# Deformable-convolution kernel: patches of 8 rows by 3 columns, hats made once per unit on compact rows and spread by transfers

## The reference, cut to what matters

```python
def _L1_conv_ref(x, w_off, b_off, w_def):      # x: group-normed input
    x = jax.nn.relu(x)
    offset = conv(x, w_off, 3x3, pad 1) + b_off        # 18 channels: (dy, dx) of 9 taps
    py = base_y + off[:, :, 0]                         # where each tap samples, per pixel
    px = base_x + off[:, :, 1]
    samp = _bilinear_gather(x, py, px)                 # 4 neighbours, bilinear weights, zero outside
    return jnp.einsum('bckhw,ock->bohw', samp, w_def)  # 9 taps x 128 channels -> 128 channels
x = x + _L1_conv_ref(_gn(x), w_off, b_off, w_def)
```

## Time and profile before

| what | us |
|---|---|
| median of 3 runs (2178.71 to 2181.53) | 2181.06 |
| the profiled execution: its span, which is its own time here | 2179.7 |
| first block | 0 to about 334 |
| first sampling product / last one | 386.8 / 2165.0 |
| PE busy over the span | 1802.6 (83%) |
| DVE | 1796.7 (82%) |
| ACT | 1445.8 (66%) |
| POOL | 1014.2 (47%) |

### The profile page before, as it was taken

The page is one execution under the profiler, slowest core; times in us unless marked ns, Lnnn a source line. Parts: engine busy times, 40 slices in busy tenths (PEclk is TensorE's granted clock), DMA queues, the critical chain, the costliest instruction groups (busy, mean ns, idle before and its releaser), DMA issues.

```text
span 2179.7 us, 38860 instructions
## 1 busy us (share of the span) xinstructions
PE 1802.6 (83%) x11347; PEld 1181.0 (54%) x11348; DVE 1796.7 (82%) x2778; ACT 1445.8 (66%) x1922; POOL 1014.2 (47%) x798
## 2 busy tenths in 40 slices
PE   5999993788888888888888888888888888888888
PEld 4877772455555555555555555555555555555545
DVE  6888875888888888888888888888888888888885
ACT  3555553677777777767676777767777767676764
POOL 2555562544444444444444444444444444444442
PEclk9999995899999999999999999999999999999999
DMA  4334332111111111111111111111111111111100
GB/s 123 116 115 120 113 90 70 43 47 43 47 47 47 47 47 47 47 44 40 45 47 47 47 46 39 47 47 47 47 47 47 47 47 46 36 47 47 47 21 20
DMA packets 129048, 120.23 MB, mean 55 GB/s; under 512 B 9257, under 2 KB 112311, under 8 KB 129015
## 3 DMA queue, kind: packets, MB, share of 16 engines
q1 hardware_dynamic: 129015, 119.82, 18.5%
HBM read 80.53 MB, written 35.71 MB: 53 GB/s over the span
## 4 chain that ended last, share of the span: by engine, by line
DVE 34%; issue 21%; PE 19%; ACT 12%; POOL 10%; DVEq 1%; ACTq 1%; DMA 0%; POOLq 0%; SPq 0%
DVE hats L1168 11%; PE bank L692 10%; ACT z L866 8%; DVE samples_lo L1178 5%; POOL weights L1466 5%; PE bank L713 5%; DVE offs L1196 5%; DVE rest L1213 4%; POOL x_bo L1421 3%; ACT dist L889 3%; DVE parts L1212 3%; DVE parts L1216 2%; PE pair L675 1%; DVE middle L1215 1%; DVE y L1248 1%
## 5 line engine op out<-in xcount | busy, mean ns | idle before, releaser
L1466 POOL TENSOR_TENSOR weights<-hats 120x512 f32<-120x512 f32 x576 | 761.1, 1326 | 959.4 <-DVE hats L1168 959.4
L889 ACT ACTIVATE dist<-pair 120x1024 f32<-120x1024 f32 x576 | 580.7, 1020 | 346.5 <-PE pair L675 204.7
L692 PE MATMUL bank<-weights,zT 120*128 120x216 f32 (+1 forms) x2816 | 621.0, 359 | 193.9 <-DVE samples_lo L1178 163.5
L692 PEld LDWEIGHTS bank<-weights,zT 120*128 120x128 f32 x2816 | 497.4, 192 | 311.3 <-DVE samples_lo L1178 285.4
L1168 DVE TENSOR_SCALAR hats<-dist 120x1024 f32<-120x1024 f32 x576 | 547.2, 951 | 53.1 <-ACT dist L889 28.5
L897 ACT ACTIVATE samples_hi<-bank 128x432 f16<-128x432 f32 (+1 forms) x704 | 358.4, 520 | 181.8 <-PE bank L692 176.9
L1178 DVE SCALAR_TENSOR_TENSOR samples_lo<-bank,samples_hi 128x432 f16<-128x432 f32 (+1 forms) x704 | 398.1, 587 | 40.9 <-ACT samples_hi L897 30.9
L675 PE MATMUL pair<-coords,select 29*120 29x512 bf16 x1152 | 240.3, 428 | 83.5 <-ACT dist L889 81.4
L713 PE MATMUL bank<-ident,z 128*120 128x128 f32 x1408 | 213.4, 288 | 41.3 <-DVE y L1248 36.9
L661 PE MATMUL bank<-samples_hi,w_hi 128*128 128x512 f16 x576 | 220.6, 383 | 1.1 <-DVE samples_lo L1178 1.1
L675 PEld LDWEIGHTS pair<-coords,select 29*120 29x120 bf16 x1152 | 71.5, 126 | 272.1 <-ACT dist L889 140.4
(11 more groups left out here) (135 smaller groups left out, 2190.0 us busy)
## 6 DMA issues: line engine op xcount, KB each, us to landing
raw<-x_pad SPq DMA_DIRECT2D x64, 690.0 KB, 4.0
x_pad<-x1g SPq DMA_DIRECT2D x64, 276.0 KB, 3.8
weights<-in_x SPq DMA_DIRECT2D x64, 256.0 KB, 3.0
x_bo<-x_pad SPq DMA_DIRECT2D x64, 256.0 KB, 3.0
out<-y SPq DMA_DIRECT2D x64, 256.0 KB, 2.1
coords<-parts SPq DMA_DIRECT2D x384, 9.0 KB
x_pad<-pad_rows SPq DMA_DIRECT2D x4, 207.0 KB, 6.3
w_defs<-in_w_def SPq DMA_DIRECT2D x1, 576.0 KB, 3.8
```

What stands on the lines that cost most here:

```text
L692: mm = nc.tensor.matmul(sampled_pair(b)[:, :, at:at + BR * cols], zT[:, u, w, :], weights[0:WPIX, u, :, w * WC * BR:(w * WC + cols) * BR], ...
L889: nc.scalar.activation(dist[0:WPIX, b], pairs[b][0:WPIX], ACT.Abs).then_inc(dist_ready, 1)
L1466: nc.gpsimd.tensor_tensor(weights[0:WPIX, u, k, :], hats[0:WPIX, b, 0, :], hats[0:WPIX, b, 1, :], ALU.mult).then_inc(weights_ready, 1)
```

## The change

A unit is now 8 rows by 64 columns, still 512 pixels, still 64 units. A window is 8 rows by 3 columns (24 pixels, 22 windows), and its source patch 14 rows by 9 columns: 126 pixels. In the patch, pixel (r, c) lies at partition 9r + c.

- **Hats.** A y hat depends only on tap and source row, an x hat only on tap and source column. So there are 14 x 9 = 126 compact rows in y and 9 x 9 = 81 in x. `locate` makes both distances of all nine taps with four fp16 products (hi and lo part of the offsets; the sum of the four 32-row parts and the constants are folded into `select`), ACT takes one absolute value, DVE makes one hats instruction, and ACT's queue stores them to HBM (hat_y, hat_x). SP then spreads them into hy_all and hx_all: for each group of three taps, a transfer of 12 rows repeated on 9 partitions each and one of 9 rows repeated 12 times, 108 partitions by 1536 fp32. The third group starts 18 partitions below the first, as a tap row down is one source row on. The rest of hy_all and hx_all stays zero from two memsets. POOL multiplies them tap by tap as before.
- **Offsets.** ACT evicts the four parts together (114 rows); DVE splits them in two instructions; the sum, the three-way split, the squares and the six small transfers are gone. The flag comes from |offset| rows in the same dist tile.
- **z.** It is stored patch by patch (22 patches of 14 x 9, with their overlaps: 128 by 2772), read from a ring of 11 blocks of 4 source rows in raw, each row loaded once per image. Near the end of the ring it takes two instructions. z_hi is 128 by 660 and reads z at a step of 9 elements.
- **Banks.** Sampling has three banks instead of two (5, 6, 7). zT has one copy instead of two, freed group by group. hy_all and hx_all have one copy, freed by group of three taps.
- **res** is gone: DVE adds x from raw. Two units share one store of 8 full rows.
- **Order.** A new ORDER, and no loop: all units are written out, with constants in the waits.
- In the first block DVE has some more memsets and small copies (for `select`), and SP a few small transfers.

```diff
-BR, WC = 4, 6
+BR, WC, UW = 8, 3, 64
...
+        hat_rows = [nc.dram_tensor("hat_y", [AHEAD, TROWS, SRC_R, CHUNK], F32, kind="Internal").ap(),
+                    nc.dram_tensor("hat_x", [AHEAD, TROWS, SRC_C, CHUNK], F32, kind="Internal").ap()]
...
+        z = sb("z", [P, 2, WINDOWS, SRC_R, SRC_C])
...
+            "z0 z1 s0 s1 c0 k0 T0 h0 s2 c1 k1 s3 T1 O0 k2 c2 s4 P0 k3 s5 T2 c3 Q0 k4 s6 G0 c4 k5 s7 H0 "
+            "T3 k6 c5 s8 c6 R0 k7 s9 T4 c7 c8 k8 s10 T5").split()]
...
+            ahead = {"c": -1, "s": 0, "k": 1, "T": 1, "z": 2, "h": 2, "O": 2, "P": 2, "Q": 2,
+                     "G": 2, "H": 2, "R": 2}
...
+            def spread_hats(n):
+
+
+                sp.wait_ge(*hats_landed(n))
+                for g in range(TROWS):
+                    wait(sp, weights_ready, TAPS * (n - 1) + TROWS * (g + 1))
+                    rows = [hat_rows[0][n % AHEAD, g, g:g + NEAR_R].rearrange("(r o) c -> r o c", o=1),
+                            hat_rows[1][n % AHEAD, g].rearrange("(o r) c -> o r c", o=1)]
+                    for dst, src in zip((hy_flat, hx_flat), rows):
+                        sp.dma_start(dst[g * SRC_C:(g + NEAR_R) * SRC_C,
+                                         g * CHUNK:(g + 1) * CHUNK],
+                                     src.broadcast_to([NEAR_R, SRC_C, CHUNK])
+                                     ).then_inc(hat_in[g], 16)
...
+            def locate(n, u, _):
+
+                pe.wait_ge(off_split, n + 1)
+                wait(pe, dist_ready, n)
+                for axis in range(2):
+                    nc.tensor.matmul(pairs[0][:, axis, :], select[:, axis, :],
+                                     offs_hi[:], start=True, stop=False)
+                    mm = nc.tensor.matmul(pairs[0][:, axis, :], select[0:CONST_AT, axis, :],
+                                          offs_lo[0:CONST_AT, :], start=False, stop=True)
+                mm.then_inc(located, 1)
...
+            def make_hats(n, u, _):
+
+                dve.wait_ge(dist_ready, n + 1)
+                if n > 0:
+                    dve.wait_ge(*hats_landed(n - 1))
+                nc.vector.tensor_scalar(hats[:], dist[:], -1.0, 0.0, ALU.add,
+                                        ALU.min).then_inc(hats_ready, 1)
...
+            dve.wait_ge(pad_out, 16 * 3 * IMGS)
+            nc.vector.memset(hx_flat, 0.0).then_inc(hats_cleared, 1)
+            for r in range(BATCH):
+                dve.wait_ge(x1_out[r], 16 * GROUPS // BATCH)
+            nc.vector.memset(hy_flat, 0.0).then_inc(hats_cleared, 1)
...
+                if k % TROWS == 0:
+                    pool.wait_ge(hat_in[k // TROWS], 32 * n + 32)
                 if k == 0:
                     wait(pool, sampled, PAIRS * (n - 1))
```

More of the change, by code:

```diff
@@ L56 @@
 KROWS = CONE + CROWS
+AXIS_ROWS = 32
+OWN = 3 * TAPS
 PIXEL_SCALE, WEIGHT_TOP = 128.0, 8192.0
@@ L181, in preact_conv_kernel @@
-        dist = sb("dist", [P, 2, 2, BW])
-        hats = sb("hats", [P, 2, 2, BW])
+        raw = sb("raw", [P, RING * RB, PADC])
+        far_raw = raw[:, 0:SRC_R, :].rearrange("p r w -> p (r w)")
+        z_hi, z_lo = (sb(n, [P, UW + 2, BR + 2], F16) for n in ("z_hi", "z_lo"))
+        offs4 = sb("offs4", [P, BW])
+        offs_hi, offs_lo = (sb(n, [SUM_ROWS, BW], F16) for n in ("offs_hi", "offs_lo"))
+        farthest = sb("farthest", [P, BANDS])
+        dist = sb("dist", [P, 2, BW])
+        hats = sb("hats", [P, 2, BW])
@@ L205, in preact_conv_kernel @@
         row_shift = sb("row_shift", [P, 1])
-        row_in = sb("row_in", [P, WW])
-        row_z = sb("row_z", [P, WW])
-        row_zT = sb("row_zT", [P, P])
-        far_dist, far_hats, far_weights = dist[:, 0], hats[:, 0], weights[:, 1, 0]
+        middle = ramps[0:NOFF]
+        parts = sb("parts", [P, BW], BF16)
+        offs, rest = hy_all[0:NOFF, 0], hy_all[0:NOFF, 1]
+        row_in, row_z, row_zT = (hy_all[:, 2, i * P:(i + 1) * P] for i in range(3))
+        far_dist, far_hats, far_weights = hx_all[:, 0:2], hx_all[:, 2:4], weights[:, 1, 0]
         samples = weights[:, 0]
@@ new lines, in _ @@
+            for block in range(RING):
+                load_block(block)
+            sp.wait_ge(hats_cleared, 2)
+            spread_hats(0)
+            spread_hats(1)
+            for n in range(BANDS + 2):
+                if n >= 2 and n % SIDES == 1:
+                    store_y(n - 2)
+                for block in range(IMGS * BLOCKS):
+                    if last_unit(block) == n - 2:
+                        load_block(block + RING)
+                if n + 2 < BANDS:
+                    spread_hats(n + 2)
@@ new lines, in distances, with store_hats @@
+            def distances(n, u, _):
+                act.wait_ge(located, n + 1)
+                wait(act, hats_ready, n)
+                wait(act, reached, n)
+                nc.scalar.activation(dist[:], pairs[0][:], ACT.Abs).then_inc(dist_ready, 1)
+            def store_hats(n, u, _):
+                wait(act, hats_ready, n + 1)
+                for axis, rows in enumerate((Y_ROWS, X_ROWS)):
+                    act.dma_start(hat_rows[axis][n % AHEAD].rearrange("g r (k c) -> (g r k) c", k=TROWS),
+                                  hats[0:rows, axis, :]).then_inc(hat_out[n % AHEAD], 16)
```

680 lines of the change are left out of this document (327 added, 353 removed).

## The result

The changed kernel took 1849.93 us (median of 4 runs, 1837.68 to 1850.67) against 2180.1 us for the kernel before in the same job. The ratio is 0.847, with a 95% interval of 0.845 to 0.850. The forecast was 1817 us with a range of 1700 to 2010: the direction and the range held, and the point was 33 us too low.

The account below looks back on a forecast made before the run. DVE's load behind PE's bank waits was taken as the bound, with PE next. First sample at 377 plus 64 passes of 22.3 us plus 10.5, then -4 and +5, gave a span of 1815.5, so 1817 us; range 1700 to 2010.

Parts of the forecast that it names:

- What bounded the kernel before: In the steady bands: PE waits 285.4 + 163.5 us for samples_lo on DVE, whose queue is full of hats.
- PE's floor: PE's work per unit: 23.06 less 3.68 for distances plus 0.82 for `locate`, 20.2 us, a floor for the pass.
- the second rival: ACT's z_hi: its stepped read costs as much as the turned one, +0.7 us before the offsets, 1862 us; chance 0.15.
- The wait of `locate` for the split: Mid-pass on PE: `locate` waits for DVE's offset split behind s4's low part, 0.7 to 2.1 us idle, taken as 1.9.
- The spreads: Six hat transfers a unit, 3.98 MB, 9.9 to 17.5 us, taken as 13: hidden, 7 us to spare, costing nothing.
- T: Time of one unit's six hat transfers, taken as 13 us; with passes of 22.3 us it may be 20.5.
- The fourth rival: Hat transfers slow but still faster than before: 20.5 to 26 us a unit, 1830 to 2150 us; chance 0.09.
- The rule of 12 engines in 16: Hat transfers with 12 rows outermost use 12 of 16 DMA engines, which makes 9.9 us 13.2.
- The walk as a sum: One pass followed across engines: 20.2 us of PE work and some 2.1 to 2.4 idle, 22.3 us, bounds 21 and 23.
- Start and end: First block and tail: z(0) at about 341, first sampling product at 377 instead of 386.8, 10.5 us after the passes.
- PE without stalls: Rival for the pass: split short and z hidden, so 20.2 to 21 us a pass, 1683 to 1734 us; chance 0.12.
- What would show it: Signs of being right: pass near 22.3 us, PE 20.2 busy, longest wait offs_lo, no weights wait, z near 2.7, spreads 13.

Follow-up runs that it names:

- the short hats: The kernel before the change, with its nine DVE hats instructions a band cut from 1024 to 2 x 64 columns (output not the reference's): 1961.67 us, ratio 0.900.
- the write-step kernel: The changed kernel with z_hi reading runs of three neighbours of z and writing fp16 at a step of 20 bytes: 1903.78 us, ratio 0.873.
- the light spreads: The changed kernel with spreads carrying only 192 of 1536 columns, same number of transfers (output not the reference's): 1901.89 us, ratio 0.873.
- the light spreads with the early split: The changed kernel with spreads of 192 of 1536 columns and DVE's offset split directly behind the offset products (output not the reference's): 1712.76 us, ratio 0.786.

## Why the prediction was right or wrong

- **What bounded the kernel before** (DVE behind PE's bank waits): right, shown by the short hats.
- **PE's floor**, 20.2 us: 19.8 measured. **DVE**, some 13: 13.6. **ACT**, some 12: 12.2. **POOL**, 11.9: 11.8. Right.
- **z**, 2.7 us taken of 2.7 to 5.6: right, 2730 ns; the eviction of 114 rows, 777 ns against 755. These two rows of the changed kernel, for z and for z_hi:

```profile
L933 ACT ACTIVATE z<-raw,norm_band x80: 718/2730/2751, 340.6 to 1777.4; 128x2772 f32<-128x2772 f32 x48, 128x2376 f32<-128x2376 f32 x6, 128x396 f32<-128x396 f32 x6, 128x1584 f32<-128x1584 f32 x6
...
L943 ACT ACTIVATE z_hi<-z x64: 1379/1404/1424, 343.3 to 1780.0; 128x660 f16<-128x660 f32 x64
```

- **z_hi**, 0.8 us taken by L873, with 1.45 by L866 as the other bound: mis-sized. It took 1.40, as the second rival had it. The Trainium skill's rule ("SBUF — State Buffer", "Door 1: The DMA port swizzle"), told with that estimate, agrees: 1404 ns for 660 elements at a step of 36 bytes, against 878 for 780 in runs. The nearest row was picked by the length of its runs, where the step seems to decide; no run separates the two. That rival's time, 1862, lies 12 us from the measured one, but its sum isn't the whole reason: it charged the full 0.7 us to the pass, and by the write-step kernel only about half of such a delay arrives, which makes an estimate of 0.3 us a pass or 20 us.
- **The wait of `locate` for the split**, 1.9 us: right, 1.5 to 2.0. offs_lo took 1631 ns beside POOL, where L1213 had 1408.
- **The spreads**, hidden with 7 us to spare: this is the step that failed. T was taken as 13 us. In the unit shown, the third group's weights start 21.2 us after the first issue, against an assumed T + 1 = 14 (in units 8 to 55 the median is 19.7, from 16.3 to 23.3). The stored hats were given 2.1 us to land, measured on a quiet queue. Now the store is issued at 1036.53, and SP, which waits for its landing, issues at 1039.77: 3.2 us here, and up to 7.6 elsewhere. The walk's start (stores at 17 of the pass) was right: 18.0 here, 16.8 in the median. So 18.0 + 3.2 + 21.2 + 3.7 = 46.1 us, and from the first sample of two units before (1018.55) to this unit's (1064.77) it is 46.2: no cover is left, and PE waits for weights in 43 of 64 units. The 13, which is 306 GB/s, was a choice between two rows of transfers that read no row twice, and the faster of them has a DMA share of 0.98, where the spreads have three quarters. The fourth rival had this mechanism, from T = 20.5 on, with 1830 as its lowest price. The rule of 12 engines in 16 stood beside the sum and was applied to the fast end only (9.9 to 13.2 us); on the slow end it gives an estimate of 17.5 x 16 / 12 = 23.3 us, and the measured 20 lies between.
- **The walk as a sum**: 20.2 us of work and 2.1 to 2.4 idle were forecast; it is 19.8 and 2.9, of which the weights, which had been given nothing, take 1.1 to 1.3. The pass is 22.66 instead of 22.3, which is 64 x 0.36 = 23 us, the first sample is 7 us late, and 3 us are left for what follows the last sample: together the 33 us. That the sum came so near is luck in one respect. It assumed hidden spreads, and with hidden spreads this order takes 1902 us, as the light spreads showed. The walk took POOL's products as a fixed delay of offs_lo; it had no step for POOL running without gaps beside z_lo and both steps of the split.
- **Start and end**: z at 340.6 (341), first sample 383.7 (377). The late part is the spreads again.
- **PE without stalls**, 1683 to 1734: not this kernel, but the light spreads with the early split (1713) lie there. The estimate of what these waits are worth was right.
- **What would show it**: three signs failed: no PE wait for weights, POOL released by transfers well before its weights are needed, and the spreads of a unit in 13 us. In total PE's largest wait was the one for offs_lo, as said. The DMA share was not near 1 but at three quarters in mid-spread, as 12 full engines of 16 would make it.

## What to carry to other kernels

When a wait on the path is removed, ask what the waiting had kept apart. Here two waits each hid the other, and one fix alone gave -16 and +52 us where both gave -137. Count a transfer's outermost size before taking a rate from another transfer, and take landing times from a loaded queue. And when a producer becomes faster, see which engine it will now run beside.

## What the runs showed of the hardware that I had not expected

- A DVE operation with two SBUF inputs can be shut out until a burst of POOL products ends: 6.69 us median for one of 1.2, behind the running product and four more. In a similar burst of another kernel it got in after one, all 62 times.
- Spreads from overlapping pieces of 6 KB, each read 8 or 6 times by one engine, moved 15.2 and 17.2 GB/s a busy engine; different rows, or the same nine rows read once by each of 12 engines, 22.2. Twelve engines that each read one row nine times moved 25 in one stretch, and the queue with them 20.7. So many readers of one row lose nothing, and what makes the overlapping pieces slow is open.
- ACT, 128 x 660 to fp16: 1404 ns with a read step of 36 bytes in runs of 10, 3087 ns with a write step of 20 bytes in runs of 3.
- Up to 5.4 us of idle on PE in 57 of 64 units took its granted clock to 0.50, and the mean from 0.97 to 0.87 in the steady part. In the change, 1.9 us of waiting was followed by 0.50 too.
